# Normalised rows a tile a step, the first rows ahead of the weight's scale, bank copies first: an edit of order in a transformer layer's kernel

## The chip, the core and the metric

One NeuronCore of a Trainium2 chip. Time is the device time of one execution, in microseconds, as the median of several runs. A program for one core is a set of instruction streams, one for each engine: TensorE (PE in the profile, its weight loads PEld), VectorE (DVE), ScalarE (ACT), GpSimd (POOL) and SyncE (SP, which issues most transfers). Each stream runs in its own written order, and semaphores let one stream wait for another. An instruction that waits holds up everything behind it on its engine.

## What is computed

Input x has 2 images of 1024 rows of 512 numbers. With `norm` a normalisation of each row:

```python
x = x + 0.5 * ffn(norm(x))      # ffn: a second normalisation, scale, shift, a ternary weight, a bias
x = x + attention(norm(x))      # 16 heads of 32, rotary positions, a mask by blocks of 64 rows
x = x + 0.5 * ffn(norm(x))
```

The ternary weight is `clip(round(w / (mean(|w|) + eps)), -1, 1)`: the mean over the whole weight is needed before the first product with it. The attention has four projections (q, k, v, out).

## The kernel before

Rows lie as tiles of 128 rows by 512 columns; a block is four tiles (512 rows), an image b has two blocks (bl), and there are two images. To normalise a block, VectorE makes statistics of each tile (line 673, `bn_stats`), combines them (`gather`, line 684), GpSimd takes the power -1/2 (`rstd_of`, line 473), and VectorE writes the four normalised tiles (`normalize`, line 694, one TENSOR_SCALAR at line 698 for each tile). TensorE then transposes the block to columns: 16 transposes of 128 by 128, in four groups of four, one group for each 128 columns of the row (`transposed`, line 897, instruction at 899). A group takes a piece of all four tiles, and so waits for all of them. ScalarE copies a group's bank out: `columns1` and `columns3` (two activations, lines 559 and 560, with the FFN's scale and shift) for an FFN, `x_high` (line 585) for the attention. VectorE subtracts what the half-precision copy lost (`f_low`, line 706; `x_low`, line 719), since products are made of high and low parts.

**Before the loop.** VectorE does the statistics of the first block, sums the absolute weight (`weight_scale`, line 729, instruction at 731), and normalises the first block; then the second block's statistics, the threshold of the weight, its normalisation, and the rest of the weight. GpSimd prepares the bias rows (lines 482 to 488) right after the first root. TensorE's program begins with a wait for the sum (line 893) and the product that spreads it over the partitions (line 894); the transposes of both blocks and the FFN's products of image 0 follow.

**The loop of steps.** From there all engines run through the same `for k in range(LAST_STEP)`, 517 steps, and each engine's instructions at step k stand in the order in which its loop body asks for them. A step of TensorE holds at most one attention score product for the softmax (line 959, from step 118), one for the row maxima (line 977, from step 59), one or two products of the q and k projection (line 997; a unit of 10 steps in every 12), and two of v (line 1037). To these are added, by lists of step numbers, the pieces of work of the other stages:

- step `SECOND` = 18: the second block of image 0 is transposed for the attention (line 946); its tiles were normalised ahead of the loop (line 792); ScalarE's `x_high` follows at step 19, VectorE's `x_low` at step 20
- `N1_STEP`: image 1's two blocks are normalised for its first FFN, `Y1_STEP`: they are transposed, one group a step, with ScalarE one step and VectorE's `f_low` two steps later; `F1_STEP`: the products, with `ffn_update` (line 712) and fresh statistics three steps later
- `S2_STEP`, `N2_STEP`, `X_STEP`: statistics, normalising and transposing of image 1 for the attention
- `S3_STEP`, `N3_STEP`, `Y3_STEP`, `F3_STEP`: the same for image 0's second FFN

Beside these, in fixed steps after each projection unit: ScalarE copies the projection's bank (line 616), GpSimd rotates it with four operations (lines 519 to 524, two of them for line 519), ScalarE makes a half copy (line 638) and GpSimd the rest (line 528), and SyncE sends it through DRAM into the stacks qst and kst. TensorE starts the next unit only after the copy of line 616, since there is one bank for it. ScalarE also copies v (line 610). VectorE reduces each score bank to negated maxima (line 844); TensorE has three banks for these and waits for the reduction two or three units back; line 854 combines a head's maxima, and line 1117 transposes them.

In ScalarE's loop body, `x_high` and the column copies stand ahead of the copies of v and of the projection's bank. In VectorE's, the four tiles of a block stand together in one step.

Of the kernel before, what the change touches and what calls it, by code (L numbers as in the profile page):

```python
# [66 lines left out]
def macaron(nc, x, w_q, w_k, w_v, w_o, w_f, bias, gamma, beta, cos_t, sin_t, ident_in, ident16_in,  # L67
            q_rows, k_rows, spread, out):
    ctx = ExitStack()
    with ctx:  # L70
# [242 lines left out]
        N1_STEP = [24, 46]  # L313
        Y1_STEP = [28, 30, 32, 34, 51, 53, 55, 57]
        F1_STEP = [38, 41, 44, 47, 67, 70, 73, 76]
        S2_STEP = [51, 80]
        N2_STEP = [58, 85]
# [3 lines left out]
        N3_STEP = [O0_START + 47, O0_START + 95]  # L321
# [223 lines left out]
        def _(act):  # L545
# [49 lines left out]
            for k in range(LAST_STEP):  # L595
                if k == SECOND + 1:
                    for n in range(4, 8):
                        x_high(0, n)
                for n in range(8):
                    if k == Y1_STEP[n] + 1:  # L600
                        columns1(1, n)
                    if k == X_STEP[n] + 1:
                        x_high(1, n)
                    if k == Y3_STEP[n] + 1:
                        columns3(0, n)
# [5 lines left out]
                if u := proj_after(k, 1):  # L611
                    n = 4 * u[0] + u[1]
                    act.wait_ge(s_proj, n + 1)
                    if n >= 2:
                        act.wait_ge(s_rl, n - 1)
                    nc.scalar.activation(t1[:, n % 2, :], pp[:, :], ACT.Copy).then_inc(s_copy, 1)  # L616
                if e := max_head(k, MAX_PLACE + 1):
# [43 lines left out]
        def _(dve):  # L661
# [31 lines left out]

            def normalize(b, bl, n, src, dst, done):
                dve.wait_ge(s_rstd, n)
                for r in range(4):
                    at = 4 * bl + r
                    nc.vector.tensor_scalar(dst[:, r, :], src[:, r, :], mv[:, b, at, 0:1], rstd[:, b, at:at + 1],  # L698
                                            ALU.subtract, ALU.mult).then_inc(done, 1)
# [58 lines left out]
            statistics(0, 0, 1, *TWICE, blocks[0][0])  # L758
            weight_scale()
            normalize(0, 0, 1, blocks[0][0], y1[0][0], s_y1[0])  # L760
# [34 lines left out]
            for k in range(LAST_STEP):  # L795
                if k == SECOND + 2:
                    for n in range(4, 8):
                        x_low(0, n)
                if k == N1_STEP[0]:
                    normalize(1, 0, 5, blocks[1][0], y1[1][0], s_y1[1])  # L800
# [5 lines left out]
                if k == N1_STEP[1]:  # L806
                    normalize(1, 1, 6, blocks[1][1], y1[1][1], s_y1[1])
# [13 lines left out]
                for bl in range(BLOCKS):  # L821
                    if k == S2_STEP[bl]:
                        gather(1, bl, 7 + bl, *ONCE)
                    if k == N2_STEP[bl]:
# [389 lines left out]
```

## Time and profile before

| | us |
|---|---|
| median of 3 runs (lowest, highest) | 591.15 (590.01, 592.42) |
| the profiled execution | 591.55 |
| its span, first to last instruction | 589.8 |
| TensorE busy in the span | 544.5 |
| VectorE, ScalarE, GpSimd busy | 389.7, 312.2, 240.5 |

Read it so: what lies between 544.5 and the span is what can be won by better order; it stands in some twenty waits of TensorE, most of them in the first 165 us and in the last 130. A wait is named by the engine and line that ended it.

### The profile page before, as it was taken

The page shows a single profiled execution, that of the slowest core. Times are in us where ns is not written, and L with a number is a line of the kernel's source. Part 1 is how long each engine was busy: PE and PEld are TensorE (multiplying, and loading weights), DVE is VectorE, ACT ScalarE, POOL GpSimd, SP SyncE. Part 2 cuts the span into 40 slices and gives each one's busy share as a digit, 9 for nine tenths or more (in the row PEclk, how much of TensorE's full clock was granted, in tenths as well). Part 3 has the DMA queues.
Part 4 walks back from the last instruction along what each step waited for, and adds up shares of the span by engine and source line. Part 5 has one row for each costly group of instructions (what it writes and reads, how often), then busy time and mean ns, then how long its engine had stood idle before and what let it go on. Part 6 is the DMA issues. An engine that isn't in the chain of part 4 may idle for free.

```text
span 589.8 us, 10037 instructions
## 1 busy us (share of the span) xinstructions
PE 544.5 (92%) x3586; PEld 235.6 (40%) x3586; DVE 389.7 (66%) x750; ACT 312.2 (53%) x629; POOL 240.5 (41%) x200
## 2 busy tenths in 40 slices
PE   0798888897989999999999999999999998999987
PEld 0544544444434344334334334344334333433443
DVE  5989778869767567666577567567567743351574
ACT  0832445212247657656667657657746658584330
POOL 4103665444565565566567557547500100000100
PEclk9999899799999999999999999999999999999999
DMA  9922123143622234422222216325410003100013
GB/s 314 391 85 81 54 81 124 55 133 102 162 81 81 63 104 149 137 81 91 82 80 92 80 58 195 119 81 153 127 55 1 2 0 143 55 19 1 36 54 124
DMA packets 43904, 57.91 MB, mean 98 GB/s; under 512 B 3830, under 2 KB 34678, under 8 KB 42832
## 3 DMA queue, kind: packets, MB, share of 16 engines
q1 hardware_dynamic: 43420, 57.21, 29.3%
q8 instruction: 29, 0.48, 0.3%
q14 instruction: 19, 0.16, 0.1%
q10 hardware_dynamic: 436, 0.07, 0.1%
HBM read 31.97 MB, written 25.17 MB: 97 GB/s over the span
## 4 chain that ended last, share of the span: by engine, by line
PE 64%; DVE 2%; DMA 2%; ACT 2%; issue 2%; POOL 1%; SPq 0%; ACTq 0%; POOLq 0%
PE bank L1097 11%; PE bank L959 11%; PE bank L997 10%; PE bank L1107 10%; PE bank L977 9%; PE bank L919 6%; PE bank L909 5%; DMA kst<-spread 1%; DMA spread<-rhl 1%; PE bank L1117 1%; DVE qst L698 1%; PE bank L899 1%; ACT big L631 1%; PE bank L906 1%; DVE rmax L844 0%
## 5 line engine op out<-in xcount | busy, mean ns | idle before, releaser
L844 DVE TENSOR_REDUCE rmax<-bank 128x1 f32<-128x512 f32 (+3 forms) x384 | 202.5, 552 | 73.1 <-PE bank L977 68.2
L631 ACT ACTIVATE big<-bank 128x512 f32<-128x512 f32 (+3 forms) x384 | 181.5, 491 | 90.9 <-PE bank L959 85.3
L959 PE MATMUL bank<-qst,kst 106*128 106x512 f16 (+3 forms) x384 | 125.5, 328 | 3.1 <-ACT big L631 2.8
L977 PE MATMUL bank<-kst,qst 104*128 104x512 f16 (+3 forms) x384 | 124.8, 328 | 3.7 <-DMA kst<-spread 2.0
L519 POOL TENSOR_TENSOR rot<-t,sin_s 64x512 f32<-64x512 f32 x64 | 82.8, 1294 | 80.9 <-ACT t L616 78.0
L1097 PE MATMUL bank<-big,ones 128*32 128x512 f32 (+3 forms) x768 | 81.8, 498 | 0.0
L1107 PE MATMUL bank<-big,rows 128*32 128x512 f32 (+3 forms) x768 | 79.5, 486 | 0.0
L959 PEld LDWEIGHTS bank<-qst,kst 106*128 106x128 f16 x384 | 36.8, 96 | 80.5 <-issue 30.0
L528 POOL TENSOR_TENSOR rhl<-t,rhl 128x512 f16<-128x512 f32 x32 | 37.1, 1161 | 57.5 <-ACT rhl L638 57.5
L538 POOL TENSOR_TENSOR cl<-cf,ch 128x512 f16<-128x512 f32 x16 | 18.6, 1161 | 88.4 <-ACT ch L656 88.4
L997 PE MATMUL bank<-xh,wh 128*128 128x512 f16 x128 | 48.9, 383 | 4.4 <-ACT t L616 3.5
L477 POOL TENSOR_TENSOR rstd<-var_e,half_neg 128x4 f32<-128x4 f32 x12 | 13.9, 1159 | 93.8 <-DVE var_e L692 93.8
L977 PEld LDWEIGHTS bank<-kst,qst 104*128 104x128 f16 x384 | 37.7, 98 | 35.9 <-issue 4.9
L997 PE MATMUL bank<-xl,wh 128*128 128x512 f16 x128 | 43.8, 383 | 0.0
L997 PE MATMUL bank<-xh,wl 128*128 128x512 f16 x128 | 43.0, 379 | 0.0
L522 POOL TENSOR_TENSOR t<-t,cos_s 128x512 f32<-128x512 f32 x32 | 41.5, 1298 | 2.5
L524 POOL TENSOR_TENSOR t<-t,rot 128x512 f32<-128x512 f32 x32 | 41.2, 1286 | 2.5
L1107 PEld LDWEIGHTS bank<-big,rows 128*32 128x32 f32 x768 | 24.5, 110 | 37.5 <-issue 34.4
L836 DVE SCALAR_TENSOR_TENSOR mrows<-bank,mrows 8x128 f16<-8x128 f32 x32 | 8.9, 278 | 44.8 <-ACT mrows L623 44.8
L623 ACT ACTIVATE mrows<-bank 8x128 f16<-8x128 f32 x32 | 8.5, 266 | 46.7 <-PE bank L1117 46.6
L673 DVE BATCH_NORM_STATS2 stats<-rows 128x6 f32<-128x512 f32 x40 | 26.5, 686 | 5.1 <-DMA rows<-in_L_attn_x_dram 4.3
L610 ACT ACTIVATE rows<-bank 128x512 f32<-128x512 f32 x16 | 9.5, 596 | 37.1 <-PE bank L1037 37.1
(105 smaller groups left out, 696.3 us busy)
## 6 DMA issues: line engine op xcount, KB each, us to landing
spread<-rhl SPq DMA_DIRECT2D x32, 256.0 KB, 2.2
qst<-spread SPq DMA_DIRECT2D x16, 384.0 KB, 3.8
kst<-spread SPq DMA_DIRECT2D x16, 384.0 KB, 3.8
x<-rows SPq DMA_DIRECT2D x4, 1024.0 KB, 4.8
spread<-rhl SPq DMA_DIRECT2D x32, 128.0 KB, 2.1
rows<-in_L_attn_x_dram SPq DMA_DIRECT2D x3, 1024.0 KB, 14.1
xh<-ch SPq DMA_DIRECT2D x4, 512.0 KB, 5.6
xl<-cl SPq DMA_DIRECT2D x4, 512.0 KB, 6.6
```

Source lines behind the costliest of these rows:

```text
L519: pool.tensor_tensor(rot[first:first + P // 2, n % 2, :], t1[other:other + P // 2, n % 2, :], sin_s[other:other + P // 2, cols], ALU.mult) ...
L522: pool.tensor_tensor(t1[:, n % 2, :], t1[:, n % 2, :], cos_s[:, cols], ALU.mult).then_inc(s_rot, 1)
L524: pool.tensor_tensor(t1[:, n % 2, :], t1[:, n % 2, :], rot[:, n % 2, :], ALU.add).then_inc(s_rope, 1)
L528: pool.tensor_tensor(rhl[:, n % 2, 1, :], t1[:, n % 2, :], rhl[:, n % 2, 0, :], ALU.subtract).then_inc(s_rl, 1)
L631: nc.scalar.activation(probs[:, st % P_PLACES, h, 0:n], pb[u % 2][:, 0:n], ACT.Exp, scale=EXP_SCALE).then_inc(s_eb, 1)
L844: nc.vector.tensor_reduce(rmax[:, at:at + 1], a_bank(u)[:, 0:n], AX.X, ALU.max, negate=True).then_inc(s_max, 1)
L919: last = nc.tensor.matmul(o_bank[b][r][:, :], (high, low)[PASSES[a][0]][:, g, r * P:(r + 1) * P], (wh, wl)[PASSES[a][1]][:, 3, g, :], star ...
L959: nc.tensor.matmul(pb[u % 2][:, 0:n], kst[0:ROWS_B, g % SETS, h, j * P:(j + 1) * P], qst[0:ROWS_B, g % SETS, h, q0:q0 + n], start=True, st ...
L977: nc.tensor.matmul(a_bank(u)[:, 0:n], qst[0:ROWS_A, g % SETS, h, i * P:(i + 1) * P], kst[0:ROWS_A, g % SETS, h, half * HALF:half * HALF + ...
L997: last = nc.tensor.matmul(pp[:, :], wp[ww][:, m % 2, cc, og * P:(og + 1) * P], xp[xw][:, cc, m // 2 * HALF:(m // 2 + 1) * HALF], start=(n ...
L1097: last = nc.tensor.matmul(psum[h * D:(h + 1) * D, q0 - half * HALF:HALF], ones[:, 0:D], probs[:, st % P_PLACES, h, 0:n], start=(j == 0), s ...
L1107: last = nc.tensor.matmul(acc[h * D:(h + 1) * D, q0 - half * HALF:HALF], rows[g // GROUPS][:, j, (GH * og + h) * D:(GH * og + h + 1) * D], ...
```

## The change

The instructions stay the same; their order does not.

- Ahead of the loop, VectorE normalises the first block before it sums the weight.
- `normalize` is split into `normalize_tile`, and in the loop a block's four tiles go one to a step, in steps N to N + 3. The second normalisation of image 1's first FFN starts at 45 (it was 46), those for the attention at 57 and 83 (58 and 85), that of the late block at 477 (479). The second four groups of `Y1_STEP` start one step earlier each.
- The second block's four groups of transposes go one to a step (18 to 21), with `x_high` at 19 to 22 and `x_low` at 20 to 23.
- In ScalarE's loop body the copies of v and of the projection's bank come first in a step, `x_high` and the column copies behind them.

```diff
-        N1_STEP = [24, 46]
-        Y1_STEP = [28, 30, 32, 34, 51, 53, 55, 57]
+        N1_STEP = [24, 45]
+        Y1_STEP = [28, 30, 32, 34, 50, 52, 54, 56]
-        N2_STEP = [58, 85]
+        N2_STEP = [57, 83]
-        N3_STEP = [O0_START + 47, O0_START + 95]
+        N3_STEP = [O0_START + 47, O0_START + 93]
...
             for k in range(LAST_STEP):
-                if k == SECOND + 1:
-                    for n in range(4, 8):
-                        x_high(0, n)
-                for n in range(8):
-                    if k == Y1_STEP[n] + 1:
-                        columns1(1, n)
-                    if k == X_STEP[n] + 1:
-                        x_high(1, n)
-                    if k == Y3_STEP[n] + 1:
-                        columns3(0, n)
                 if (v := v_unit(k, 1)) and v[2] == 5:
...
                     nc.scalar.activation(t1[:, n % 2, :], pp[:, :], ACT.Copy).then_inc(s_copy, 1)
+                if SECOND + 1 <= k < SECOND + 5:
+                    x_high(0, k - SECOND + 3)
+                for n in range(8):
+                    if k == Y1_STEP[n] + 1:
+                        columns1(1, n)
+                    if k == X_STEP[n] + 1:
+                        x_high(1, n)
+                    if k == Y3_STEP[n] + 1:
+                        columns3(0, n)
...
+            def normalize_tile(b, bl, n, r, src, dst, done):
+                dve.wait_ge(s_rstd, n)
+                at = 4 * bl + r
+                nc.vector.tensor_scalar(dst[:, r, :], src[:, r, :], mv[:, b, at, 0:1], rstd[:, b, at:at + 1],
+                                        ALU.subtract, ALU.mult).then_inc(done, 1)
...
             statistics(0, 0, 1, *TWICE, blocks[0][0])
+            normalize(0, 0, 1, blocks[0][0], y1[0][0], s_y1[0])
             weight_scale()
-            normalize(0, 0, 1, blocks[0][0], y1[0][0], s_y1[0])
...
-                if k == SECOND + 2:
-                    for n in range(4, 8):
-                        x_low(0, n)
-                if k == N1_STEP[0]:
-                    normalize(1, 0, 5, blocks[1][0], y1[1][0], s_y1[1])
+                if SECOND + 2 <= k < SECOND + 6:
+                    x_low(0, k - SECOND + 2)
+                if N1_STEP[0] <= k < N1_STEP[0] + 4:
+                    normalize_tile(1, 0, 5, k - N1_STEP[0], blocks[1][0], y1[1][0], s_y1[1])
...
-                if k == N1_STEP[1]:
-                    normalize(1, 1, 6, blocks[1][1], y1[1][1], s_y1[1])
+                if N1_STEP[1] <= k < N1_STEP[1] + 4:
+                    normalize_tile(1, 1, 6, k - N1_STEP[1], blocks[1][1], y1[1][1], s_y1[1])
...
-                    if k == N2_STEP[bl]:
+                    if N2_STEP[bl] <= k < N2_STEP[bl] + 4:
                         dve.wait_ge(s_ytr1[1], 4 * bl + 4)
-                        normalize(1, bl, 7 + bl, blocks[1][bl], y1[1][bl], s_y2[1])
+                        normalize_tile(1, bl, 7 + bl, k - N2_STEP[bl], blocks[1][bl], y1[1][bl], s_y2[1])
...
-                    if k == N3_STEP[bl]:
+                    if N3_STEP[bl] <= k < N3_STEP[bl] + 4:
                         if bl:
                             dve.wait_ge(s_ytr3[0], 4)
-                        normalize(0, bl, 9 + bl, resid[0][bl], y3[0][bl], s_y3[0])
+                        normalize_tile(0, bl, 9 + bl, k - N3_STEP[bl], resid[0][bl], y3[0][bl], s_y3[0])
...
-                if k == SECOND:
+                if SECOND <= k < SECOND + CC:
                     pe.wait_ge(s_y2[0], 8)
-                    for cc in range(CC):
-                        transposed(x_bank[0][4 + cc], y1[0][1], cc, s_xtr[0])
+                    transposed(x_bank[0][4 + k - SECOND], y1[0][1], k - SECOND, s_xtr[0])
```

## Rows read from the trace of the kernel before

**Rows 1.** The page: busy time of each engine, share of the span, instructions.

```profile
PE 544.5 (92%) x3586; PEld 235.6 (40%) x3586; DVE 389.7 (66%) x750; ACT 312.2 (53%) x629; POOL 240.5 (41%) x200
```

**Rows 2.** Waits of PE: who waited for whom: us in total, times, longest.

```profile
PE bank L894 <- DVE sums L731: 12.0, 1, 12.0
PE bank L899 <- DVE big L698: 8.4, 3, 3.0
PE bank L997 <- ACT t L616: 3.5, 2, 2.6
PE bank L1117 <- DVE rmax L844: 3.4, 1, 3.4
...
PE bank L977 <- DVE rmax L844: 1.6, 3, 1.0
```

**Rows 3.** Timeline of the opening: start us, us, engine, line [idle before <-releaser].

```profile
7.87 1.02 POOL L477 TENSOR_TENSOR rstd<-var_e,half_neg 128x4 f32<-128x4 f32 x1 [6.29 <-DVE var_e L692]
...
9.52 2.29 DVE L731 TENSOR_REDUCE sums<-cl 128x1 f32<-128x2048 f32 x1 [1.80 <-DMA cl<-in_L_ffn_weight_dram]
...
11.73 3.15 DVE L698 TENSOR_SCALAR big<-rows,mv,rstd 128x512 f32<-128x512 f32 x4
...
12.17 0.68 POOL L486 CAST bias_rows<-cf 1x512 f16<-1x512 f32 x1
...
15.02 3.65 PE L899 MATMUL bank<-ident,big 128*128 128x128 f32 x16 [2.51 <-DVE big L698]
```

**Rows 4.** Timelines of DVE and POOL: tiles alone, and one beside a POOL operation.

```profile
41.08 1.91 DVE L698 TENSOR_SCALAR big<-rows,mv,rstd 128x512 f32<-128x512 f32 x4
...
92.27 1.49 DVE L698 TENSOR_SCALAR kst<-rows,mv,rstd 128x512 f32<-128x512 f32 x1
...
92.14 1.33 POOL L519 TENSOR_TENSOR rot<-t,sin_s 64x512 f32<-64x512 f32 x1
```

**Rows 5.** Timelines of PE, DVE, ACT and POOL, 61 to 78 us (steps 18 to 36).

```profile
61.51 3.63 PE L899 MATMUL bank<-ident,big 128*128 128x128 f32 x16 [2.98 <-DVE big L698]
...
71.24 0.60 PE L899 MATMUL bank<-ident,kst 128*128 128x128 f32 x4
...
77.90 0.38 PE L997 MATMUL bank<-xh,wh 128*128 128x512 f16 x1 [0.87 <-ACT t L616]
...
64.36 2.48 DVE L719 TENSOR_TENSOR xl<-bank,xh 128x512 f16<-128x512 f32 x4
66.76 2.86 DVE L698 TENSOR_SCALAR kst<-rows,mv,rstd 128x512 f32<-128x512 f32 x4
...
67.12 0.60 ACT L616 ACTIVATE t<-bank 128x512 f32<-128x512 f32 x1
...
67.79 2.95 POOL L519 TENSOR_TENSOR rot<-t,sin_s 64x512 f32<-64x512 f32 x2 [2.24 <-ACT t L616]
```

**Rows 6.** Timelines of PE and ACT, 96 to 108 us (steps 51 to 62).

```profile
96.36 0.60 PE L899 MATMUL bank<-ident,kst 128*128 128x128 f32 x4
...
104.09 0.39 PE L997 MATMUL bank<-xh,wh 128*128 128x512 f16 x1 [2.63 <-ACT t L616]
...
105.77 0.96 PE L899 MATMUL bank<-ident,kst 128*128 128x128 f32 x4 [0.90 <-DVE kst L698]
107.74 0.58 PE L977 MATMUL bank<-kst,qst 104*128 104x512 f16 x1 [1.00 <-DVE rmax L844]
...
98.33 0.63 ACT L638 ACTIVATE rhl<-t 128x512 f16<-128x512 f32 x1
```

**Rows 7.** Timelines of DVE at step 85 and of PE at step 481.

```profile
136.37 4.61 DVE L698 TENSOR_SCALAR kst<-rows,mv,rstd 128x512 f32<-128x512 f32 x4
...
520.19 0.66 PE L899 MATMUL bank<-ident,qst 128*128 128x128 f32 x4 [0.85 <-DVE qst L698]
```

**Rows 8.** Windows: start:end, us, busy (count) PE PEld DVE ACT POOL, PEclk, DMA share, GB/s.

```profile
61.61:65.01 3.40, 3.40 (x17) 3.34 (x18) 3.32 (x12) 1.79 (x3) 1.48 (x2) 0.50 0.34 116
141.60:145.00 3.40, 3.16 (x20) 2.04 (x21) 2.54 (x6) 1.40 (x4) 0.13 (x1) 1.00 0.01 1
```

More of the change, by code:

```diff
@@ L692, in gather @@
                 nc.vector.tensor_scalar(var_e[:, b, cols], mv[:, b, cols, 1], mul, add, ALU.mult, ALU.add).then_inc(s_var, 1)
+            def normalize_tile(b, bl, n, r, src, dst, done):
[3 more added lines that the diff above has]
+                                        ALU.subtract, ALU.mult).then_inc(done, 1)
             def normalize(b, bl, n, src, dst, done):
-                dve.wait_ge(s_rstd, n)
                 for r in range(4):
-                    at = 4 * bl + r
-                    nc.vector.tensor_scalar(dst[:, r, :], src[:, r, :], mv[:, b, at, 0:1], rstd[:, b, at:at + 1],
-                                            ALU.subtract, ALU.mult).then_inc(done, 1)
+                    normalize_tile(b, bl, n, r, src, dst, done)
             def f_low(n, f_full, f_high, f_lo, ready, done):
```

## The prediction

> **What bounds the kernel now.** I read the page first: TensorE is busy 92% of the span, VectorE 66%, ScalarE 53%, GpSimd 41% [rows 1]. So the time is TensorE's work plus the stretches in which it has none, and an edit off TensorE counts only where it shortens or lengthens such a stretch. Then the waits of TensorE [rows 2]: 12.0 us for the first reduction, 8.4 in three waits for normalised rows, 3.5 in two for ScalarE's bank copy, 3.4 in one and 1.6 in three for the reductions of the maxima. Then the timeline around each edit. The change adds and removes no instruction; it only moves them, so everything below is a matter of who waits where.
>
> **One price first: a normalised tile beside GpSimd.** A tile is one VectorE TENSOR_SCALAR from SBUF to SBUF. With GpSimd idle four take 1.91 us. Beside a GpSimd operation one takes 1.49, and it ends 0.28 after that operation (92.14 + 1.33 = 93.47, against 92.27 + 1.49 = 93.76) [rows 4]. So where GpSimd works without a pause, one tile gets through per GpSimd operation, about every 1.41 us (I take 1.33 and a gap of 0.08; the two of [rows 5] take 2.95). A reduction or subtraction from PSUM shows no such stretch: four x_low take 2.48 [rows 5]. GpSimd has such work in fixed bursts: four operations after every ScalarE copy of the projection's bank (line 616), from 0.07 after it (67.12 + 0.60, then 67.79).
>
> **1. First rows ahead of the weight's scale (lines 758 to 760).** Now the reduction runs 9.52 to 11.81, the four tiles 11.73 to 14.88 [rows 3]. After, the tiles can begin when GpSimd's root ends, 7.87 + 1.02 = 8.89. But GpSimd's four bias operations start then. The first tile gets in; three each wait for one, the last for the one that begins at 12.17 and takes 0.68: 12.85 + 0.28 = 13.13. The reduction then ends at about 13.05 + 2.29 = 15.34, where VectorE was free at 14.88: 0.46 later, and VectorE's chain (statistics, threshold, second rows, columns' low parts) decides when the first FFN product starts. TensorE gains nothing from early tiles: its program waits for the reduction (line 893) before any transpose, so with its first product behind it the transposes start some tenths after 15.34 instead of at 15.02. I take **+0.5**; bounds -0.6 (no stretch at all; VectorE idles 0.6 less) and +1.7 (GpSimd's first bias operation wins and all four tiles wait).
>
> **2. The second block's columns, steps 18 to 28.** TensorE's wait of 2.98 before 61.51 [rows 5] stays: each single transpose group still waits for all four tiles (s_y2 at 8), and the tiles it waits for lie ahead of the loop, unmoved. The 16 transposes are the same work, only spread. What moves is ScalarE's part. The copy of V (step 20) and the bank copy (step 22) now come ahead of x_high of columns 5 and 7, so the last x_high starts after the bank copy of 67.12 and ends near 68.2 (0.60, as that copy); TensorE's step 24 waits for it at 68.2, which is when it arrives: nothing. x_low of the last column (0.62 apiece) ends near 68.9. Before, the four x_low ran 64.36 to 66.84 and the tiles 66.76 to 69.62, three of them ahead of GpSimd's burst of 67.79. After, all four fall into it: GpSimd's operations end near 69.1, 70.5, 71.9 and 73.3, so the last tile ends near 73.6. TensorE wants these rows at 71.24 (step 28): a new wait of 2.4. Behind it the columns, the copies of ScalarE and the bank copy that TensorE waits for at 77.90 follow nearly back to back, so little is won back: some tenths, where ScalarE now waits for GpSimd's sum. I take **+2.1**; bounds 0 (the tiles get through before the burst) and +2.4.
>
> **3. Second half of image 1, steps 45 to 62.** The third tile still ends at 92.27 + 1.49 = 93.76 [rows 4], but now update 2 and its statistics (VectorE, step 47) go between it and the fourth, which misses a GpSimd operation and ends two rounds later, 96.5. TensorE is to transpose at step 50, one step (0.7: the eight steps from 71.24 to 77.90 take 6.66, 0.87 of it waiting) ahead of the 96.36 of [rows 6]. It arrives at 95.7, waits, and starts near 96.5: +0.2 instead of -0.7. On ScalarE the half copy of 0.63 at 98.33 filled a wait for the transposes; with the steps moved it stands behind the next two column copies, costs some 0.5 there, and the bank copy that ends TensorE's 2.63 wait at 104.09 comes at about +0.7. Now the tiles of steps 57 to 60. The first follows f_low of column 6; f_low of column 7 (step 58) stands ahead of the second, and ends within 0.1 of GpSimd's next burst. Three tiles then wait one GpSimd operation each, 0.28 after ends of 1.33, 2.74 and 4.15: 4.4 after the burst's start at 104.8, that is 109.2. TensorE wants them for the transposes that began at 105.77. It wins back the 1.00 in front of 107.74 [rows 6], since the maxima get through between the tiles. 109.2 + 0.96 = 110.2 against 107.74: **+2.4** for steps 45 to 62. Bounds: +0.9 (the second tile beats the burst, one round less), +2.6.
>
> **4. Steps 83 to 86.** Now four tiles hold VectorE from 136.37 for 4.61, and TensorE's 3.4 wait for a maximum ends only then [rows 2, 7]. After, a maximum follows each tile, and the wait needs the one behind the third tile. But the tiles begin two steps (1.4) earlier, where GpSimd's burst also runs, and the small SBUF minimum of line 854 falls among them and waits for a round of its own: 136.37 - 1.4 + 4 x 1.41 = 140.6, where the fourth tile now ends at 140.98. I take **-0.4**; bounds -1.8 (one round less) and +0.5. SP and GpSimd issue nothing new here; GpSimd's roots move one or two steps earlier past no other operation of its queue.
>
> **5. Late tiles.** At step 431 the tiles keep their start; of the 1.6 in three waits, 1.00 is that of 107.74, and I take half the rest, **-0.3** (0 to -0.6). At step 477 two tiles go ahead of an FFN update that now precedes them all; the fourth ends before TensorE arrives, and the 0.85 before 520.19 [rows 7] goes: **-0.8** (0 to -0.85). Next in line there are ScalarE's column copies, which move with the transposes.
>
> **Sum:** 0.5 + 2.1 + 2.4 - 0.4 - 0.3 - 0.8 = +3.5. The profiled execution took 591.55, 0.4 above the median of the three runs, 591.15; from it 595.05, on the median's scale **594.6 us** (594.65). A run of this kernel can tell about 0.5%, 3.0 us, from no change: below 588.2 is faster, above 594.1 slower. The forecast lies just past that edge.
>
> **A rule against a row.** [Rows 4] show that a tile which got in beside GpSimd did not hold GpSimd up: its operation beside a tile took 1.33, and four operations stay within their burst. The Trainium skill, SBUF — State Buffer (SBUF: two separate sides), says the pair of ports shared by the two is an exclusive lock for a whole instruction and that the loser fully blocks. That agrees with the tile's wait, but by it GpSimd would also lose a tile's time per round, which the row does not show.
>
> **The rivals.**
> *Faster: the maxima get through.* Place: the tiles of steps 57 to 60 and 83 to 86. If they find GpSimd between bursts, TensorE loses neither 0.90 nor 1.00 near 106, nor more than 1 of the 3.4, and with 0.85 at the end and nothing at step 28 that is -(1.9 + 2.4 + 0.8) + 0.5 = -4.6: 586.5. It decides as soon as a tile is asked for before the bank copy has ended. For it: the waits are really there [rows 2, 6]. Against: every tile group stands within two steps of such a copy. Chance 0.12.
> *One of the two losses does not come.* Either at step 28 or at step 61 the tiles slip ahead: +3.5 - 2.1 = +1.4, 592.5, or +3.5 - 1.5 = +2.0, 593.1. For it: at step 58 the race is 0.1 wide. Chance 0.28.
> *The clock.* After the wait of 2.98 the granted clock was 0.50 from 61.6 to 65.0 [rows 8], that is 1.2 instead of 2.4 GHz; a wait of 2.4 at step 28 may do the same. 3.4 us at half speed lose 1.7, of which TensorE's 0.87 in front of 77.90 hides part: +1.0, 595.6. Against it: after the 3.4 wait near 140 it was 1.00 [rows 8]. Chance 0.10.
> *GpSimd is held for a whole tile.* Then each round lasts 0.46 longer, four at step 28 and three at step 60: +3.2, 597.8. Chance 0.06. This is what the lock of SBUF — State Buffer in the Trainium skill would do if it bound both sides.
> *The change does not do what it says* holds for part 1 and is in the sum.
>
> **How the numbers follow.** Forecast 0.44, its own range 592.5 to 596. Of it 0.28 lies above 594.1; with clock and lock that makes slower 0.44. The single loss and the rest of the forecast are within 0.5%: 0.46 with a little of the faster rival; faster 0.10. The range 589.8 to 597.2 takes in both single-loss cases and the clock, and leaves out most of the faster rival and the lock.
>
> **What would show it.** Right: the transposes at step 28 waiting 2 us or more for VectorE's kst rows, each tile before it near 1.4 to 1.5; first transposes later than 15.02; the wait before 61.51 still near 3; that for the qst rows near 520 gone. Wrong: tiles of 0.54 at steps 24 to 27 or 57 to 60, a first wait of TensorE shorter than 12 followed by early transposes, or the 3.4 wait near 140 down to 1.

## The result, and the profile after

The changed kernel takes 592.79 us (median of 20 runs) against 590.83 (20 runs) of the kernel before: 1.003 times as long, 95% interval 1.0017 to 1.0044, that is +1.8 us (1.0 to 2.6). The forecast was +3.5. The direction is right, the forecast about twice what came, and by the forecast's own bound of 0.5% the change is within "no change". One of the 20 runs of the changed kernel took 716.31 at a mean granted clock of 0.754, and one of six of the kernel with both tile groups moved, below, took 594.80; the ratios leave both out. The profiled execution took 593.34 with a span of 591.6 (before 591.55 and 589.8), so the two traces differ by as much as the medians, and can be set side by side instruction by instruction.

By the page of the kernel after no count of instructions moved, and TensorE is busy for 545.0 us, 0.5 longer than in [rows 1]; what differs is who waits. The waits of TensorE after: us in total, times, longest (answers to [rows 2]; lines have shifted by one or two: 895, 900, 733 and 696 are 894, 899, 731 and 698 of before, and the bank copy, 616 of before, is now 606):

```profile
PE bank L895 <- DVE sums L733: 14.2, 1, 14.2
PE bank L900 <- DVE kst L696: 6.0, 3, 3.1
PE bank L900 <- DVE big L696: 5.5, 2, 3.0
PE bank L997 <- ACT t L606: 3.4, 2, 2.5
...
PE bank L977 <- DVE rmax L845: 1.9, 2, 1.2
...
PE bank L1117 <- DVE rmax L845: 0.6, 1, 0.6
```

Read it against [rows 2]. The wait for the sum is longer by 2.2 and those for normalised blocks (big) shorter by 2.9: TensorE waits for the sum alone, where it waited for the sum and then again for the first block. The waits for kst rows, of which the list of before held a single one of 0.9 ([rows 6] has it), are now three with 6.0 (2.19, 3.09 and 0.68, at steps 28, 61 and 50): the loss. The wait of 3.4 for a maximum fell apart into smaller ones (0.6, and two of those at line 977), and that for the qst rows near 520 is not in the list: the gains.

**The opening.** Timelines of VectorE, GpSimd and TensorE after: start us, us, engine, line, operation [idle before <- releaser] (answer to [rows 3]; the second line, one of the four tiles, is from a narrower window):

```profile
9.39 2.49 DVE L696 TENSOR_SCALAR big<-rows,mv,rstd 128x512 f32<-128x512 f32 x4 [1.20 <-POOL rstd L477]
10.61 0.53 DVE L696 TENSOR_SCALAR big<-rows,mv,rstd 128x512 f32<-128x512 f32 x1
11.81 2.27 DVE L733 TENSOR_REDUCE sums<-cl 128x1 f32<-128x2048 f32 x1
...
9.53 2.07 POOL L482 TENSOR_SCALAR bias_rows<-cf 1x512 f16<-1x512 f32 x1 [0.17 <-POOL rstd L477]
...
14.22 0.56 PE L895 MATMUL bank<-sums,ones 128*128 128x1 f32 x2 [14.22 <-DVE sums L733]
14.64 3.61 PE L900 MATMUL bank<-ident,big 128*128 128x128 f32 x16
```

The four tiles do not wait for one bias operation each. They are through in 2.49: the fourth ends at 11.88, 0.28 after line 482 (9.53 + 2.07 = 11.60), and the three ahead of it got through before that: the third ran from 10.61 to 11.14 while line 482 was under way. Timelines of GpSimd and VectorE before:

```profile
9.06 1.49 POOL L482 TENSOR_SCALAR bias_rows<-cf 1x512 f16<-1x512 f32 x1 [0.17 <-POOL rstd L477]
...
12.93 1.20 POOL L488 TENSOR_TENSOR bias_rows<-cf,bias_rows 1x512 f16<-1x512 f32 x1
...
13.05 1.37 DVE L698 TENSOR_SCALAR big<-rows,mv,rstd 128x512 f32<-128x512 f32 x1
```

With no tile beside it line 482 took 1.49. Line 488, on one partition too, does hold a tile to its end: 13.05 + 1.37 = 14.42, 0.29 after 12.93 + 1.20 = 14.13. The sum, which in [rows 3] began after 1.80 of idling for the weight's transfer, now follows the tiles without a gap, and VectorE is through with both at 14.08 instead of 14.88. That 0.8 goes down its chain: the first FFN product starts at 25.63, before at 26.44.

**Steps 18 to 28.** Timelines of VectorE, GpSimd and TensorE after (answer to [rows 5]):

```profile
67.84 0.69 DVE L721 TENSOR_TENSOR xl<-bank,xh 128x512 f16<-128x512 f32 x1 [1.02 <-ACT xh L585]
68.45 4.75 DVE L696 TENSOR_SCALAR kst<-rows,mv,rstd 128x512 f32<-128x512 f32 x4
...
67.40 2.71 POOL L519 TENSOR_TENSOR rot<-t,sin_s 64x512 f32<-64x512 f32 x2 [3.51 <-ACT t L606]
...
71.59 1.32 POOL L524 TENSOR_TENSOR t<-t,rot 128x512 f32<-128x512 f32 x1
...
59.85 1.12 PE L900 MATMUL bank<-ident,big 128*128 128x128 f32 x4 [3.00 <-DVE big L696]
...
73.25 0.66 PE L900 MATMUL bank<-ident,kst 128*128 128x128 f32 x4 [2.19 <-DVE kst L696]
```

The wait of 3.0 at step 18 stays. All four tiles of step 24 fall into GpSimd's burst (the burst is the run of four operations from line 519 to 524), 4.75 us where [rows 5] have 2.86, and the last ends at 73.20, 0.29 after line 524 (71.59 + 1.32). TensorE, there at 71.06, waits 2.19 at step 28, where it waited for nothing. Something else went on as well: the granted clock. Windows of the kernel after, columns as in [rows 8]:

```profile
59.04:62.44 3.40, 2.59 (x9) 1.79 (x10) 3.36 (x11) 1.23 (x2) 1.17 (x2) 0.50 0.16 54
62.44:65.84 3.40, 3.40 (x14) 2.33 (x13) 1.22 (x6) 1.43 (x3) 1.02 (x1) 0.50 0.37 106
```

After the wait at step 18 the clock was 0.50 (1.2 GHz) for 6.8 us; [rows 8] show it for 3.4. TensorE came to step 18 with a lead of 1.66 and had 0.18 of it at step 28, with the same products to do: the low clock took 1.5.

**Steps 57 to 62.** Timelines of VectorE, GpSimd and TensorE after (answer to [rows 6]):

```profile
105.70 0.54 DVE L696 TENSOR_SCALAR kst<-rows,mv,rstd 128x512 f32<-128x512 f32 x1
...
107.04 2.89 DVE L696 TENSOR_SCALAR kst<-rows,mv,rstd 128x512 f32<-128x512 f32 x2
...
110.06 1.28 DVE L696 TENSOR_SCALAR kst<-rows,mv,rstd 128x512 f32<-128x512 f32 x1
...
106.96 2.69 POOL L519 TENSOR_TENSOR rot<-t,sin_s 64x512 f32<-64x512 f32 x2 [2.49 <-ACT t L606]
...
106.94 0.61 PE L997 MATMUL bank<-xh,wh 128*128 128x512 f16 x1 [2.51 <-ACT t L606]
...
111.39 1.11 PE L900 MATMUL bank<-ident,kst 128*128 128x128 f32 x4 [3.09 <-DVE kst L696]
112.30 0.63 PE L977 MATMUL bank<-kst,qst 104*128 104x512 f16 x1
```

The second tile was asked for at 107.04, 0.08 after the burst had begun, so that three tiles pay a round each and the transposes of step 61 wait 3.09 instead of 0.90. The 1.00 in front of the next maxima product is gone, as the forecast had it.

**Late.** Timeline of TensorE, the first line before, the others after (answer to [rows 7] and to the wait of 3.4 in [rows 2]):

```profile
164.99 0.38 PE L977 MATMUL bank<-kst,qst 104*128 104x512 f16 x1 [1.70 <-DMA kst<-spread]
...
142.81 0.39 PE L977 MATMUL bank<-kst,qst 104*128 104x512 f16 x1 [0.69 <-DVE rmax L845]
...
144.44 0.27 PE L1117 MATMUL bank<-ident,rmax 128*8 128x128 f32 x1 [0.59 <-DVE rmax L845]
145.88 0.23 PE L977 MATMUL bank<-kst,qst 104*128 104x128 f16 x1 [1.18 <-DVE rmax L845]
...
168.33 0.38 PE L977 MATMUL bank<-kst,qst 104*128 104x512 f16 x1 [1.21 <-DMA kst<-spread]
...
521.92 0.66 PE L900 MATMUL bank<-ident,qst 128*128 128x128 f32 x4
```

One wait of 3.4 became three of 2.5 in sum, the wait for a transfer near 165 fell from 1.70 to 1.21, and the one near 520 is gone.

The ledger, from the starts of the same TensorE instruction in both traces (after minus before):

| stretch | us |
|---|---|
| up to the first FFN product | -0.80 |
| first FFN, to step 18 | -0.86 |
| steps 18 to 36: new wait 2.2, clock 1.5 | +3.68 |
| steps 36 to 62 | +2.54 |
| steps 83 to 88 | -0.78 |
| transfer near 165 | -0.44 |
| near 211 | -0.16 |
| step 431 | -0.53 |
| step 477 | -0.92 |
| to the end | +0.06 |
| sum | +1.79 |

The second line is the clock too. Timelines of TensorE in the first FFN, the first line before, the others after:

```profile
28.52 1.91 PE L909 MATMUL bank<-wt,xl 128*128 128x512 f16 x4
...
26.01 1.91 PE L910 MATMUL bank<-wt,xh 128*128 128x512 f16 x4
...
29.10 1.03 PE L910 MATMUL bank<-wt,xh 128*128 128x512 f16 x4
```

After, four products took 1.91 while the granted clock was 0.50 (window 25.20 to 28.30) and 1.03 at 1.00. Before, they still took 1.91 at 28.52 and came to the faster rate only near 30.9; the windows list 1.00 there, but the products' own times say that it was the lower level. In the other traces the faster rate comes anywhere between the first product and 31.7 us, with either order of the opening, so the 0.86 is no part of the edit. Against it stands the 1.5 that the low clock took after step 18; without both, this pair of traces would differ by some 1.2.

### The profile page after: what moved, and what is told of

Same layout as the page of the kernel before. It is cut to its first block, busy times and chain, and to the rows that moved or that the text cites. A ratio compares the mean times of both kernels' runs of the same rounds, so it can differ in the third digit from the quotient of the medians.

```text
span 591.6 us, 10046 instructions
## 1 busy us (share of the span) xinstructions
PE 545.0 (92%) x3586; PEld 235.0 (40%) x3586; DVE 390.6 (66%) x750; ACT 311.8 (53%) x629; POOL 240.3 (41%) x200
## 4 chain that ended last, share of the span: by engine, by line
PE 65%; DMA 2%; ACT 2%; issue 1%; POOL 1%; DVE 1%; SPq 0%; ACTq 0%; POOLq 0%
PE bank L1097 12%; PE bank L959 11%; PE bank L1107 10%; PE bank L997 10%; PE bank L977 9%; PE bank L920 6%; PE bank L910 5%; DMA kst<-spread 1%; PE bank L1117 1%; DMA spread<-rhl 1%; ACT big L630 1%; PE bank L900 1%; PE bank L907 1%; POOL rot L519 0%; DVE cl L708 0%
```

## The experiments

The theory: the change is four edits whose costs add, each set by whether a tile meets GpSimd's burst. The rivals: the clock made the loss, GpSimd was held up, or the order of ScalarE's copies did it. Ratios are to the kernel before, run beside each group.

### Each part alone

**First rows ahead of the sum, alone.**

```diff
-            weight_scale()
             normalize(0, 0, 1, blocks[0][0], y1[0][0], s_y1[0])
+            weight_scale()
```

> Kernel before with the opening alone changed: the first block's rows are normalised ahead of the weight's sum. By the prediction's term: four tiles in about 4.2 us, three of them waiting for a GpSimd operation, +0.5 us. By the theory from the trace after: the tiles take 2.5 us because two of them pass while GpSimd's first bias operation is held (2.07 instead of 1.49 us), the transposes start 0.8 to 0.9 us earlier counted from the first root's end, and the first FFN product 1.3 us earlier; total -1.3 us.

Measured: 590.5 (12 runs), 0.999 [0.9971, 1.001], that is -0.6 with 1.2 to either side. By the time alone this settles nothing; +0.5 lies just at the end of the interval. The trace tells more. Timelines of VectorE and GpSimd of this kernel:

```profile
9.95 2.49 DVE L697 TENSOR_SCALAR big<-rows,mv,rstd 128x512 f32<-128x512 f32 x4 [1.20 <-POOL rstd L477]
...
10.07 2.08 POOL L482 TENSOR_SCALAR bias_rows<-cf 1x512 f16<-1x512 f32 x1 [0.16 <-POOL rstd L477]
```

Tiles of 2.49 and a bias operation of 2.08, as in the full change. The start of the first FFN product wanders from execution to execution, since the first rows and the weight land at different times; over all profiled executions of this study it began at 26.44 to 27.20 in the five with the old order (mean 26.66), and at 25.63 to 26.61 in the nine with the new (mean 26.04). That is about 0.6. Counted from the end of the first root it is clearer: 16.27 (within 0.01) in all nine with the new order, 17.55 in four with the old and 17.93 in the fifth, so the edit shortens this stretch by 1.28, as the expectation had it. But the root ended at 9.76 in the mean of the nine and at 9.04 in that of the five, which takes 0.7 back; whether the edit has a part in that is not shown. In this kernel the product came at 26.18, 0.26 sooner than before, and the -1.3 expected of the total is not shown.

**The second block alone** (with the tiles of steps 24 to 27 and ScalarE's bank copies first; the diff is shortened).

```diff
+                if SECOND + 1 <= k < SECOND + 5:
+                    x_high(0, k - SECOND + 3)
...
+                if N1_STEP[0] <= k < N1_STEP[0] + 4:
+                    normalize_tile(1, 0, 5, k - N1_STEP[0], blocks[1][0], y1[1][0], s_y1[1])
...
+                if SECOND <= k < SECOND + CC:
                     pe.wait_ge(s_y2[0], 8)
+                    transposed(x_bank[0][4 + k - SECOND], y1[0][1], k - SECOND, s_xtr[0])
```

> Kernel before with the second block's transposes and columns a step apart, its tiles at steps 24 to 27, and the bank copies first. By the prediction: a wait of 2.2 to 2.4 us for VectorE at step 28, three or four tiles of 1.4 to 1.5 us before it, total +2.1 us. By the rival that the growth between steps 18 and 36 in the trace after (3.7 us) is the clock's share of 1.5 us and would have gone otherwise: the same wait, but a total that follows the granted clock of steps 18 to 28: +0.6 to +1.2 us where the low stretch stays at 3.4 us, +3.7 us where it is 6.8.

Measured: 597.4 (6 runs), 1.01 [1.0073, 1.0126], +5.9 us: far above +2.1, so something the theory had not priced. Timeline of TensorE, GpSimd and VectorE near step 61:

```profile
112.51 1.12 PE L903 MATMUL bank<-ident,kst 128*128 128x128 f32 x4 [5.08 <-DVE kst L696]
...
106.68 2.69 POOL L519 TENSOR_TENSOR rot<-t,sin_s 64x512 f32<-64x512 f32 x2 [1.60 <-ACT t L606]
...
106.76 5.70 DVE L696 TENSOR_SCALAR kst<-rows,mv,rstd 128x512 f32<-128x512 f32 x4
```

The order of ScalarE's copies shows here by itself. With the bank copy ahead of step 58's column copies, GpSimd's burst starts at 106.68, 0.08 before the four tiles, which this kernel still keeps in one step: they take 5.70 and TensorE waits 5.08. The shorter wait for the bank copy (1.30 instead of 2.63) is lost several times over. In the full change the first of these four tiles goes a step earlier, at step 57, and gets in ahead of the burst, so three tiles pay there and not four. The clock has a share too. Window of this kernel, columns as in [rows 8]:

```profile
74.82:78.22 3.40, 3.40 (x12) 1.77 (x11) 0.76 (x2) 2.70 (x5) 1.15 (x1) 0.50 0.00 0
```

The granted clock was 0.50 for 3.4 us after step 18 and again here, behind the wait at step 28, where TensorE fell back by 1.6. The expectation by the clock (+0.6 to +1.2 with 3.4 us after step 18) missed as well. The parts are not independent: ScalarE's order decides where the burst lies.

**The second block with ScalarE's old order.** The test of that reading: the same kernel with the column copies ahead of the bank copies, as before.

```diff
+                if SECOND + 1 <= k < SECOND + 5:
+                    x_high(0, k - SECOND + 3)
                 for n in range(8):
                     if k == Y1_STEP[n] + 1:
                         columns1(1, n)
...
                 if (v := v_unit(k, 1)) and v[2] == 5:
```

> Kernel before with the second block's transposes and columns a step apart and tiles at steps 24 to 27, but ScalarE's column copies ahead of the bank copies as before (the run of the second block had the bank copies first and took 5.9 us more than before). If the tiles at step 28 alone made those 5.9: the same here. If the bank copy ahead of the column copies of step 58 took the rest, because GpSimd's burst then starts ahead of the tiles of that step: the wait of 2.2 at step 28 stays, the one at step 61 falls back to about 0.9, total +2.1 us.

Measured: 594.74 (6 runs), 1.0064 [1.0043, 1.0086], +3.8 us. TensorE's waits for kst rows in this kernel's list:

```profile
PE bank L903 <- DVE kst L696: 3.2, 2, 2.3
```

The wait at step 61 is back at 0.9, so ScalarE's order made the 5.08; the wait at step 28 stays at 2.3 without it, so that one is the tiles' own. The time is 1.7 above the +2.1, and why is not shown. In its trace the granted clock was 0.50 for 6.8 us after step 18, as in the kernel after, where the kernel before has 3.4; but this profiled execution took 593.26, the shortest of the six and only 2.0 above the median before, so its low clock does not account for the median.

**Steps 45 to 60 alone.**

```diff
-        N1_STEP = [24, 46]
-        Y1_STEP = [28, 30, 32, 34, 51, 53, 55, 57]
+        N1_STEP = [24, 45]
+        Y1_STEP = [28, 30, 32, 34, 50, 52, 54, 56]
-        N2_STEP = [58, 85]
+        N2_STEP = [57, 85]
```

> Kernel before with the tiles of steps 45 to 48 and 57 to 60 and the four transposes from step 50 alone. By the prediction: the wait for the bank copy at step 60 stays, a wait of 2.5 to 3.5 us for VectorE's tiles at step 61, total +2.4 us. By the rival that the low clock around 106 to 113 us decides: waits as said, total anywhere from +1 to +4 us with the length of the low stretch (6.8 us before, 10.2 after).

Measured: 593.52 (12 runs), 1.0044 [1.0024, 1.0063], +2.6 us, against +2.4 forecast. The granted clock was 0.50 from 104.7 to 111.6, 6.8 us as in the kernel before, so the rival that a longer low stretch makes the loss falls. Its wait for kst rows at step 61 is 3.67:

```profile
108.43 1.12 PE L905 MATMUL bank<-ident,kst 128*128 128x128 f32 x4 [3.67 <-DVE kst L697]
```

**The late tiles alone.**

```diff
-        N2_STEP = [58, 85]
+        N2_STEP = [58, 83]
-        N3_STEP = [O0_START + 47, O0_START + 95]
+        N3_STEP = [O0_START + 47, O0_START + 93]
```

> Kernel before with the tiles of steps 83 to 86, 431 to 434 and 477 to 480 alone. By the prediction: -1.5 us (0.4, 0.3 and 0.8). By the theory from the trace after: the 3.4 us wait near step 87 falls to about 2.5 us in pieces and gives 1.8, the transfer behind it 0.4, the two late places 0.7 and 0.9: -3.5 us or a little more, faster than before by 0.6%.

Measured: 588.46 (12 runs), 0.9957 [0.9938, 0.9975], -2.5 us (-3.7 to -1.5), against -1.5 forecast. Its trace has the same three waits at steps 85 to 88 as the full change (0.69, 0.59 and 1.18). By starts of equal instructions: -0.6 at steps 83 to 88, -0.35 at the transfer near 163, -0.5 at step 431, -0.9 at step 477. Each term is a little more than forecast, and the transfer was not in the sum. The -3.5 that the trace after had suggested lies near the end of the interval.

### Parts taken back from the full change

**The second block and the tiles of step 24 clumped again.**

```diff
-                if N1_STEP[0] <= k < N1_STEP[0] + 4:
-                    normalize_tile(1, 0, 5, k - N1_STEP[0], blocks[1][0], y1[1][0], s_y1[1])
+                if k == N1_STEP[0]:
+                    normalize(1, 0, 5, blocks[1][0], y1[1][0], s_y1[1])
...
-                if SECOND <= k < SECOND + CC:
+                if k == SECOND:
```

> Kernel after with the second block's transposes and columns and the tiles of step 24 put back in one step each; all else as after. By the theory (the four tiles fall into GpSimd's burst): the 2.2 us wait at step 28 goes and the total falls by 2.2 us, to about the time before. By the rival that the clock made the difference: the wait goes, but the total falls by 0.7 or 3.7 us with the low stretch around 60 us at 3.4 or 6.8 us.

Measured: 590.81 (12 runs), 0.9993 [0.9977, 1.0009]. Against the full change (+1.8) that is -2.2: in place the second block costs about what the forecast gave it, 2.1. The wait at step 28 is gone. By the rival of the clock the total should have fallen by 0.7 or 3.7; with some 1.2 to either side of the 2.2 both lie outside, the smaller only just. The parts now add: -0.6 + 2.2 + 2.6 - 2.5 = +1.7, where +1.8 was measured; with some 1 us to either side of each part, that they meet to 0.1 is luck. The +3.8 of the same edit made alone is 1.6 more than the 2.2, with some 1.8 to either side, so the two are not shown to differ.

**Only the tiles of step 24 moved, to step 20.** If the burst makes the loss, tiles that are done before it need not be given up.

```diff
-        N1_STEP = [24, 45]
+        N1_STEP = [20, 45]
...
-                    if k == N1_STEP[bl] - 2:
+                    if k == (22, 43)[bl]:
```

> Kernel after with the tiles of image 1's first block at steps 20 to 23 instead of 24 to 27, between the subtractions of the second block's columns; GpSimd's root stays at its step. If the burst is the cause: two or three tiles take 0.54 us, the last is done near 69.5 us on the trace after, the wait at step 28 falls from 2.2 to under 0.3, total -2.2 us, the time before. If the late columns of ScalarE themselves are the cause, the last tile still waits behind the last column and the wait stays above 1.5 us.

Measured: 590.39 (12 runs), 0.9987 [0.9971, 1.0003], 2.5 below the full change. Timeline of VectorE and GpSimd of this kernel:

```profile
64.89 0.54 DVE L696 TENSOR_SCALAR kst<-rows,mv,rstd 128x512 f32<-128x512 f32 x1
...
65.94 0.54 DVE L696 TENSOR_SCALAR kst<-rows,mv,rstd 128x512 f32<-128x512 f32 x1
...
67.21 0.68 DVE L696 TENSOR_SCALAR kst<-rows,mv,rstd 128x512 f32<-128x512 f32 x1
...
66.16 2.85 POOL L519 TENSOR_TENSOR rot<-t,sin_s 64x512 f32<-64x512 f32 x2 [3.51 <-ACT t L606]
```

Three of the tiles start before the burst at 66.16 and cost 0.54 or 0.55; the fourth takes 0.68. The wait at step 28 is gone, though the transposes are still spread and the granted clock was still 0.50 for 6.8 us (57.8 to 64.6). So it is the place of the tiles, not the spreading and not the clock, that makes these 2.2.

**Only the tiles of step 57 moved, to step 53.**

```diff
-        N2_STEP = [57, 83]
+        N2_STEP = [53, 83]
```

> Kernel after with the tiles of steps 57 to 60 at 53 to 56, ahead of GpSimd's burst that follows the bank copy of step 58. If the burst is the cause: tiles of 0.54 us, the 3.1 us wait at step 61 falls under 0.5, total -2 to -2.5 us. If the wait is set by ScalarE's columns or by the maxima, the wait moves to one of those and the total falls by less than 1 us.

Measured: 590.43 (12 runs), 0.9989 [0.9966, 1.0012], 2.4 below the full change. TensorE's timeline at step 61:

```profile
107.35 1.06 PE L900 MATMUL bank<-ident,kst 128*128 128x128 f32 x4
```

No wait stands in front of it, where the full change has 3.09.

**Both moved.**

```diff
-        N1_STEP = [24, 45]
+        N1_STEP = [20, 45]
-        N2_STEP = [57, 83]
+        N2_STEP = [53, 83]
```

(with the root kept at step 22, as above)

> Kernel after with both moves (tiles at steps 20 to 23 and at 53 to 56). If both losses are as the theory has them and add: -4.5 us against after, some 588 us, 0.4 to 0.5% faster than before. If the second loss was only a consequence of the first, no more than the larger of the two single moves.

Measured: 586.21 (6 runs), 0.9921 [0.9897, 0.9945]: 4.7 below the kernel before, 6.5 below the full change, where the two alone sum to 4.9. With half widths of 1.4 and 0.8 on the two sides, more than additive is not shown. This is faster than both kernels.

### Towards a better order

**The next waits near 96 and 104**: in step 47 the fourth tile ahead of the FFN update, in step 53 the half copy ahead of the column copies.

```diff
+                if (u := proj_after(k, 8)) and k == 53:
+                    n = 4 * u[0] + u[1]
...
-                if N1_STEP[1] <= k < N1_STEP[1] + 4:
+                if N1_STEP[1] <= k < N1_STEP[1] + 3:
...
+                if k == N1_STEP[1] + 2:
+                    normalize_tile(1, 1, 6, 3, blocks[1][1], y1[1][1], s_y1[1])
```

> The kernel with both tile groups early, and two small changes of order: the fourth tile of step 48 goes into step 47 ahead of the update, and at step 53 ScalarE's half copy goes ahead of the column copies. By the prediction's part 3 (the fourth tile costs 0.8 at step 50, the half copy some 0.5 on the way to the bank copy of step 58): the wait of 0.69 us at step 50 goes and the bank copy comes 0.5 to 1.1 us earlier, total -0.7 to -1.1 against the kernel with both early. If the bank copy hangs on ScalarE's whole chain from the first transposes alone, the total falls by no more than 0.6.

Measured: 585.78 (6 runs), 0.9909 [0.9881, 0.9936]; the 0.4 below the kernel with both tiles moved is too little to tell. Timelines of TensorE of this kernel, and in the last line of the kernel with both tiles moved:

```profile
102.77 0.39 PE L1005 MATMUL bank<-xh,wh 128*128 128x512 f16 x1 [2.00 <-ACT t L606]
...
106.63 0.38 PE L985 MATMUL bank<-kst,qst 104*128 104x512 f16 x1 [1.66 <-DMA kst<-spread]
...
108.27 0.58 PE L977 MATMUL bank<-kst,qst 104*128 104x512 f16 x1 [0.88 <-DMA kst<-spread]
```

Both edits did locally what they should: the wait of 0.69 at step 50 is gone and the one for the bank copy is 2.00 instead of 2.51. Four us later TensorE waits 1.66 for a transfer for which it waited 0.88 before; even so it is there 1.64 sooner (106.63 against 108.27). That the median shows only 0.4 of this is not explained.

**The second block's statistics and tiles ahead of the first burst.**

```diff
+            dve.wait_ge(s_up1[0], 6)
+            tile_statistics(1, 0, blocks[0][1])
-            for n in range(4):
-                weight_low(2, n)
-            statistics(0, 1, 4, *ONCE, blocks[0][1])
+            for r in range(1, 4):
+                tile_statistics(1, r, blocks[0][1])
+            gather(0, 1, 4, *ONCE)
```

(the low parts of two weights follow behind the tiles)

> The kernel with both tile groups early; besides, ahead of the loop, the second block's statistics follow its updates and its four tiles come before the last four low parts of a weight, ahead of GpSimd's first burst near 55 us. By the theory that a tile's price is GpSimd's burst: these four tiles take about 1.9 instead of 4.7 us, TensorE's wait of 2.98 at step 18 falls under 0.5, total -2.5 to -3; with the granted clock staying at 1.00 after it, 1 to 1.7 more. By the rival that VectorE's backlog sets that wait, whatever the order: the wait stays above 2 and moves to the weight's low parts or a later stage.

Measured: 584.88 (6 runs), 0.9892 [0.9866, 0.9918], the lowest median of all, 6.4 below the kernel before; the two kernels beside it differ from it by less than their intervals. Timelines of VectorE and TensorE of this kernel:

```profile
51.45 1.90 DVE L696 TENSOR_SCALAR big<-rows,mv,rstd 128x512 f32<-128x512 f32 x4
...
51.59 0.61 PE L1041 MATMUL bank<-wl,xh 128*128 128x512 f16 x2 [2.66 <-DVE wl L751]
```

The tiles are as fast as with GpSimd idle (1.90 against the 1.91 of [rows 4]) and the wait of 3.0 at step 18 is gone. But VectorE makes the low parts of a weight later, and TensorE waits 2.66 for those: the backlog of VectorE moves the wait rather than removing it, and the low clock moves with it (0.50 from 52.7 to 56.1). What is left, 1.3 below the kernel with both tiles moved, is within the two intervals.

**Both of these.**

```diff
+            dve.wait_ge(s_up1[0], 6)
+            tile_statistics(1, 0, blocks[0][1])
...
+                if (u := proj_after(k, 8)) and k == 53:
```

> Both of the two foregoing kernels' changes together. If their gains lie at different waits of TensorE they add: 4 to 5 us less than the kernel with both tile groups early, some 582 us, 1.5% under before. If not, the time of the better of the two.

Measured: 585.73 (6 runs), 0.9905 [0.988, 0.9931]. Nothing is added: the waits for the low parts (2.7 in all), the bank copy (2.9) and the transfers (2.7) are those of the two kernels it is made of.

## Why the prediction was right in its direction and wrong in its size

**Part 1 failed in its sign.** The step that failed is "three each wait for one": the forecast took the round of one tile per GpSimd operation from [rows 4], a 128-partition operation inside a burst, and applied it to the bias operation of line 482. There only the fourth tile waited for the end of the operation, and line 482 gave way, lasting 2.07 in place of the 1.49 that it took in the trace of before. That it has one partition is not the reason, since line 488 has one too and held its tile; what sets line 482 apart is not shown. The tiles took 2.49, not the 4.2 that the steps give, the reduction started at 11.81 instead of 13.05, with the root done 0.47 later than the forecast had taken from [rows 3], and the +0.5 became about -0.6: the time alone says -0.6 with 1.2 to either side, the traces say that the first product comes 0.6 sooner. The sign named in the forecast, first transposes later than 15.02, failed: they began at 14.64. The lower bound, -0.6 with VectorE's idling for the weight gone, is where it came out.

**Part 2 held.** Forecast: last tile near 73.6, wait 2.4, cost +2.1, the wait of 3.0 at step 18 unmoved. Measured: 73.20, 2.19, +2.2 in place, 3.00. Moving nothing but these tiles takes the wait and the cost away, so the mechanism is shown. The row given for "no such stretch" [rows 5] lies ahead of the burst; the kernel after has the case itself, a subtraction of 0.69 at 67.84 beside line 519.

**Part 3 held.** Forecast +2.4, measured +2.6 alone, and 2.4 back when the tiles of step 57 move. The small wait at step 50 came as 0.68, where the steps give 0.8 (95.7 to 96.5). The race at step 58, called 0.1 wide, was lost by 0.08; the wait of 1.00 behind it went, as foreseen.

**Part 4 was mis-sized by some tenths.** -0.4 forecast, -0.6 to -0.8 measured; the maxima did get between the tiles. The line 854 minimum waited its round as foreseen (1.02 us at 140.94). Not in the sum at all was the wait for a transfer near 165: it fell by 0.35 to 0.44, and why it is shorter was not tried.

**Part 5 was mis-sized.** Step 431: -0.3 forecast, -0.5 measured in both kernels. Step 477: -0.8 forecast, -0.9 measured. Together parts 4 and 5 were forecast at -1.5; alone they gave -2.5 (-3.7 to -1.5).

**The sum.** +3.5, less 1.1 for part 1 and about 1.0 for parts 4 and 5, is +1.4; +1.8 was measured. The forecast of 594.6 came out too high by part 1, whose sign it had wrong, and by the late terms, of which it took that of step 431 at half and that of the transfer not at all.

**The rivals.** Neither loss stayed away, so that rival did not come, though the time landed where it had pointed (592.5): luck, and nothing for that rival. The clock came in part, in this trace in another place than named: the low stretch after the wait at step 18 was twice as long, +1.5, against which the first FFN, sooner at the faster rate, sets 0.86. In the kernels that keep the second block clumped the low stretch was 3.4 us in each trace; of the seven that spread it and still wait there, three had 6.8 and four had 3.4. It also came where the rival had put it, behind the wait at step 28, in two of the four kernels that have this wait: for 3.4 us each in the second block alone (74.82 to 78.22, 1.6 lost) and in the kernel with the tiles of step 57 moved (72.2 to 75.6, 1.7 lost). And the row against that rival was one trace: after the like wait near 140 the clock was 0.50 for 3.4 us in three others that have it (both kernels of the second block and that of steps 45 to 60). What decides between these was not settled.
## What to carry to other kernels

Spreading a clump of VectorE work over steps helps where other work of VectorE was queued behind the clump (the maxima at step 85), and hurts where the clump was just early enough to get ahead of a GpSimd burst (steps 24 and 58): look where GpSimd's next burst begins before choosing the step. Four steps earlier for two groups of tiles turned +1.8 into -4.7 us. A price taken from one pair of operations is not the price of another pair on the same two engines: here the bounds went from -0.6 to +1.7, and the sign of the term was not known until the pair itself had been run. Count a stretch from the event that starts it, as from the end of the first root here, when what comes ahead of it differs from execution to execution.

## What was not expected of the hardware

- Tiles and GpSimd hold each other up differently by the operation. Inside a burst of 128- and 64-partition operations one tile passes per operation, each 0.28 to 0.33 us after its end, and GpSimd pays 0.06. At line 482, on one partition, three of four tiles had passed before its end, and it paid 0.58 (2.07 and 2.08 in the nine traces with the new order, 1.48 or 1.49 in the five with the old); at line 488, on one partition too, the tile waited for the end.
- A tile asked for just ahead of a GpSimd operation delays that operation: line 522 took 1.52 where the tile had started 0.14 earlier, against 1.27 without a tile. Timelines of VectorE and GpSimd of the kernel after:

```profile
140.94 1.02 DVE L855 TENSOR_TENSOR rmax<-rmax 128x4 f32<-128x4 f32 x1
141.88 0.53 DVE L696 TENSOR_SCALAR kst<-rows,mv,rstd 128x512 f32<-128x512 f32 x1
...
142.02 1.52 POOL L522 TENSOR_TENSOR t<-t,cos_s 128x512 f32<-128x512 f32 x1
```

- After a like wait at step 18 (2.98 to 3.00) the clock stayed at 0.50 for 3.4 us in some traces and for 6.8 in others, worth 1.5 to 1.7 us of 590. After the shorter waits at step 28 (2.2 to 2.3) it was 0.50 for 3.4 us in two traces of four.
